# Cross-attention in a perceiver block: steps reordered, and the wide key half changes TensorE column tiles every two batches

## What is computed

```python
def cross_attn(x, context, Wq, Wk, Wv):
    Q = x @ Wq
    K, V = (context @ Wk, context @ Wv)
    energy = jnp.einsum('bqd,bkd->bqk', Q, K)
    Sk = energy.shape[-1]
    lengths = jnp.sum(energy[:, 0] != 0, axis=-1)
    pad = kidx[None, None, :] >= lengths[:, None, None]
    energy = jnp.where(pad, NEG_INF, energy)
    score = jax.nn.softmax(energy / np.sqrt(DK), axis=-1)
    return jnp.einsum('bqk,bkd->bqd', score, V)
```

## Time and profile before

| | |
|---|---|
| median of three runs | 1068.92 us |
| the profiled execution | 1062.33 us, its span 1060.4 us |
| TensorE busy | 1031.4 us, 97% of the span |
| VectorE, ScalarE, GpSimd busy | 577.9, 391.1, 198.7 us |
| granted TensorE clock, mean | 0.994 |
| moved by DMA | 206.93 MB |

### The profile page before, as it was taken

One profiled execution on the slowest core, in us unless ns is written; L12 is line 12 of the kernel. 1 busy time (PEld: TensorE's weight loads), 2 busy tenths in 40 slices (PEclk: granted clock), 3 DMA queues, 4 the chain that ended last, 5 costly groups with the idle time before them and its releaser, 6 DMA issues.

```text
span 1060.4 us, 14025 instructions
## 1 busy us (share of the span) xinstructions
PE 1031.4 (97%) x5263; PEld 768.1 (72%) x5263; DVE 577.9 (55%) x1111; ACT 391.1 (37%) x622; POOL 198.7 (19%) x180
## 2 busy tenths in 40 slices
PE   8999899999999999899999999999999999999998
PEld 4454444444444467788888888899999999999997
DVE  4056333324333448798645666767555665556556
ACT  2111122111111223335567662444444444444441
POOL 2002400000000046535522224630000000000041
PEclk9999999999999989999999999999999999999999
DMA  9934199989999922103421100684554545544453
GB/s 304 400 125 171 77 364 400 380 358 401 416 404 407 377 65 59 40 20 100 126 63 40 40 11 8 230 299 146 179 197 147 187 145 186 184 147 168 145 154 135
DMA packets 38567, 206.93 MB, mean 195 GB/s; under 512 B 5313, under 2 KB 6849, under 8 KB 34289
## 3 DMA queue, kind: packets, MB, share of 16 engines
q1 hardware_dynamic: 33312, 187.98, 48.4%
q0 software_dynamic: 5200, 18.22, 4.8%
HBM read 190.07 MB, written 16.12 MB: 194 GB/s over the span
## 4 chain that ended last, share of the span: by engine, by line
PE 88%; DVE 6%; DMA 2%; POOL 2%; issue 1%; ACT 1%; SPq 0%; DVEq 0%; ACTq 0%
PE ps L632 22%; PE ps L850 21%; PE ps L866 11%; PE ps L559 8%; PE ps L585 8%; PE ps L443 7%; DMA big<-in_ctx 2%; PE ps L463 1%; DVE big L1349 1%; PE ps L543 1%; PE ps L450 1%; PE ps L587 1%; PE ps L891 1%; DVE big L1354 1%; DVE stats L1219 1%; PE ps L569 1%
## 5 line engine op out<-in xcount | busy, mean ns | idle before, releaser
L850 PE MATMUL ps<-x,w 128*128 128x320 f32 x1536 | 237.2, 310 | 1.1 <-DVE x L1750 1.1
L850 PEld LDWEIGHTS ps<-x,w 128*128 128x128 f32 x1536 | 228.5, 188 | 5.1 <-issue 1.4
L1700 DVE TENSOR_TENSOR w<-big,w 128x1536 fp32r<-128x1536 f32 x64 | 112.4, 1758 | 91.7 <-ACT w L1143 91.2
L1805 POOL TENSOR_TENSOR u<-big,u 128x512 fp32r<-128x512 f32 (+1 forms) x44 | 64.0, 1463 | 364.1 <-ACT u L983 364.1
L866 PE MATMUL ps<-w,hsplit 128*128 128x512 f32 x512 | 128.9, 394 | 0.0
L1143 ACT CAST w<-big 128x1536 fp32r<-128x1536 f32 x64 | 94.4, 1478 | 40.2 <-PE ps L866 40.2
L559 PE MATMUL ps<-big 128*64 128x512 f32 (+2 forms) x512 | 103.2, 505 | 2.4 <-DVE ps L1343 1.1
L866 PEld LDWEIGHTS ps<-w,hsplit 128*128 128x128 f32 x512 | 93.3, 188 | 16.6
L632 PE MATMUL ps<-xcT,u 128*128 128x512 f32 x432 | 98.2, 389 | 0.0
L632 PEld LDWEIGHTS ps<-xcT,u 128*128 128x128 f32 x432 | 81.0, 188 | 17.0 <-DVE xcT L1488 0.2
L443 PE MATMUL ps<-big 128*128 128x512 f32 x208 | 90.5, 594 | 0.9 <-ACT big L932 0.9
(11 more groups left out here) (280 smaller groups left out, 1367.7 us busy)
## 6 DMA issues: line engine op xcount, KB each, us to landing
big<-in_ctxT SPq DMA_DIRECT2D x16, 3202.0 KB, 14.2
big<-in_ctx SPq DMA_DIRECT2D x16, 3072.0 KB
big<-in_w_units SPq DMA_DIRECT2D x64, 768.0 KB, 4.3
big<-in_dense_units SPq DMA_DIRECT2D x42, 256.0 KB, 2.7
xs<-big POOLq DMA_DIRECT2D x1, 5120.0 KB, 24.4
big<-in_gate_units SPq DMA_DIRECT2D x12, 384.0 KB, 3.0
hr<-xs SPq DMA_DIRECT2D x7, 512.0 KB, 5.2
ys<-big POOLq DMA_DIRECT2D x7, 512.0 KB, 3.3
```

The lines of the kernel that those rows point to most:

```text
L850: mm = nc.tensor.matmul(ps[:, 2 * part + f % 2, 0:SLOTS], wsplit[f % RING][w][:, c:c + P], xsplit[j][x][:, d, :], start=(d == 0 and w + x ...
L1700: V.tensor_tensor(wsplit[f % RING][1][:], wraw[f % RING], wsplit[f % RING][0][:].bitcast(F32), ALU.subtract).then_inc(w_low, 1)
L1805: G.tensor_tensor(low[:, 0:w], uraw[u % 4][:, 0:w], high[:, 0:w].bitcast(F32), ALU.subtract).then_inc(u_low, 1)
```

## The change

- The wide half sits in column tile 0 for batches 0, 1, 4, 5, ... and in tile 1 for 2, 3, 6, 7, ... (`WIDE`); its matmuls are issued first. The narrow half's pad in PSUM is on the other partitions after each switch, so it is written anew every second batch, with -1e38 instead of 0. Pad columns then count as nonzero, and a small constant `sides` corrects count and key index (one more subtraction in `shift`, and a subtraction in place of a copy in `exchanged`).
- `values` is issued in two parts: its first two key tiles before the exchange, the other four and the tail after.
- The late queries are issued in halves over steps 1 to 7 (`LATE`), the third chunk whole in step 5.
- The output of n-2 is transposed without folding (four 128-column transposes). VectorE then adds the two halves (`output_sum`) between the count and the reading of the exchange, into a buffer that shares memory with two later tiles; ScalarE and VectorE take high and low parts from there.
- The first rows of the product by Wv no longer wait for the outputs of batches 14 and 15; the transposes of batch 15 come after row 1. ScalarE rounds four weight units, not two, ahead of the last output copy.

```diff
@@ -36,6 +36,8 @@
 NEG = -1e38
 FLOOR = -5e37
 PIECES = ((0, 512, 512), (512, KA - 512, KH * P - 512))
+WIDE = [n // 2 % 2 for n in range(B)]
+LATE = {1: (0, 0, 2), 2: (0, 2, 4), 3: (1, 0, 2), 4: (1, 2, 4), 5: (2, 0, 4), 6: (3, 0, 2), 7: (3, 2, 4)}
 ATANH_TERMS = 9
...
-        fold = sb("fold", [P, S])
...
-        oh = sb("oh", [P, NT * TOPK, NE])
-        rk = sb("rk", [P, NT * TOPK, NE])
+        pair = sb("oh_rk", [P, 2, NT * TOPK * NE])
+        oh, rk = (pair[:, k, :].rearrange("p (n e) -> p n e", e=NE) for k in range(2))
+        osum = pair[:].rearrange("p k (c q) -> p (k c) q", q=S)
-        s_work = sb("s_work", [P, 2, 12])
+        s_work = sb("s_work", [P, 2, 13])
+        sides = sb("sides", [P, 2, 4])
...
-            def late_queries(c):
-
-                pe.wait_ge(late_out, 8)
-                if c:
-                    pe.wait_ge(late_q_out, c)
-                for d in range(DC):
+            def late_queries(c, lo, hi):
+
+                if lo == 0:
+                    pe.wait_ge(late_out, 8)
+                    if c:
+                        pe.wait_ge(late_q_out, c)
+                for d in range(lo, hi):
                     mm = nc.tensor.matmul(ps[:, 1, :], m2[:, d, tok(c)], late2T[d], start=(d == 0), stop=(d == DC - 1))
-                mm.then_inc(late_q, 1)
+                if hi == DC:
+                    mm.then_inc(late_q, 1)
...
                 if n:
                     pe.wait_ge(shifted, n)
-                else:
-                    pe.wait_ge(pad_cleared, 1)
+                if n % 2 == 0:
+                    pe.wait_ge(pad_cleared, n // 2 + 1)
                 for piece, (lo, *widths) in enumerate(PIECES):
                     for d in range(DC):
-                        for half in range(2):
-                            col, w = half * KA + lo, widths[half]
+                        for half in (WIDE[n], 1 - WIDE[n]):
+                            narrow = half != WIDE[n]
+                            col, w = narrow * KA + lo, widths[narrow]
                             mm = nc.tensor.matmul(ps[half * S:half * S + S, 2 + piece, 0:w], qT[:, d, n * S:(n + 1) * S],
                                                   cT[n % 2][:, d, col:col + w], start=(d == 0), stop=(d == DC - 1))
                 mm.then_inc(e_done, 1)
...
-            def values(n):
+            def values(n, lo, hi):
 
                 j = n % 2
-                pe.wait_ge(nat_in[j], 32 * (n // 2 + 1))
-                pe.wait_ge(pt_evac[0], n + 1)
-                pe.wait_ge(pt_evac[1], 2 * n + 2)
-                if n:
-                    pe.wait_ge(o_copied, n)
-                for t in range(KH):
-                    for half in range(2):
+                if lo == 0:
+                    pe.wait_ge(nat_in[j], 32 * (n // 2 + 1))
+                    pe.wait_ge(pt_evac[0], n + 1)
+                    if n:
+                        pe.wait_ge(o_copied, n)
+                else:
+                    pe.wait_ge(pt_evac[1], 2 * n + 2)
+                for t in range(lo, hi):
+                    for half in (WIDE[n], 1 - WIDE[n]):
+                        narrow = half != WIDE[n]
                         mm = nc.tensor.matmul(ps[half * S:half * S + S, 6, :], pts[:, t, half * S:half * S + S],
-                                              nat[j][:, half * KH + t, :], start=(t == 0), stop=(half == 1 and t == KH - 1))
-                mm = nc.tensor.matmul(ps[0:S, 6, :], pts[0:TAIL, KH, 0:S], nat[j][0:TAIL, KT, :], start=False, stop=True)
-                mm.then_inc(pv_done, 1)
+                                              nat[j][:, narrow * KH + t, :], start=(t == 0), stop=(narrow and t == KH - 1))
+                if hi == KH:
+                    w = slice(WIDE[n] * S, WIDE[n] * S + S)
+                    mm = nc.tensor.matmul(ps[w, 6, :], pts[0:TAIL, KH, w], nat[j][0:TAIL, KT, :], start=False, stop=True)
+                    mm.then_inc(pv_done, 1)
 
             def transpose_output(n):
 
                 pe.wait_ge(o_copied, n + 1)
                 if n:
-                    pe.wait_ge(o_evac, n)
+                    pe.wait_ge(o_evac, 2 * n - 1)
                 for d in range(DC):
-                    mm = nc.tensor.matmul(ps[:, 7, d * S:(d + 1) * S], osb[:, d * P:(d + 1) * P], fold[:],
-                                          start=True, stop=True)
+                    mm = nc.tensor.transpose(ps[:, 7, d * P:(d + 1) * P], osb[:, d * P:(d + 1) * P], ident[:])
                 mm.then_inc(o_done, 1)
...
                     transpose_probabilities(n - 1)
                 if n >= 2:
                     transpose_output(n - 2)
+                if n:
+                    values(n - 1, 0, 2)
                 exchange(n)
                 if n == 0:
                     late_transposes()
-                if 3 <= n < 3 + DC:
-                    late_queries(n - 3)
+                if n in LATE:
+                    late_queries(*LATE[n])
                 if n:
-                    values(n - 1)
-            transpose_output(B - 1)
+                    values(n - 1, 2, KH)
...
-            pe.wait_ge(o_evac, B)
-            for i in range(6):
+            pe.wait_ge(o_evac, 2 * (B - 2))
+            value_rows(0)
+            value_rows(1)
+            transpose_output(B - 1)
+            value_rows(2)
+            pe.wait_ge(o_evac, 2 * B - 1)
+            for i in range(3, 6):
                 value_rows(i)
             split_transposes("t2", 0)
             split_transposes("t2", 1)
             value_rows(6)
             split_transposes("t2", 2)
             split_transposes("t2", 3)
+            pe.wait_ge(o_evac, 2 * B)
             value_rows(7)
             pe.wait_ge(fb_low, 2)
             fc1_half(0)
...
             def output_out(n):
-                act.wait_ge(o_done, n + 1)
-                nc.scalar.copy(oT_high[:, :, n * S:(n + 1) * S],
-                               ps[:, 7, 0:DC * S].rearrange("p (c q) -> p c q", q=S)).then_inc(o_high, 1)
+                act.wait_ge(o_evac, 2 * n + 1)
+                nc.scalar.copy(oT_high[:, :, n * S:(n + 1) * S], osum[:]).then_inc(o_high, 1)
...
-                    if 3 <= n < 3 + DC:
-                        late_queries_out(n - 3)
+                    if n in LATE and LATE[n][2] == DC:
+                        late_queries_out(LATE[n][0])
                     if n == B:
-                        for u in range(2):
+                        for u in range(DC):
                             unit_high(u)
                     output_copy(n - 1)
                 if n == 3:
                     nc.scalar.copy(fbias[:], lnw[:, 6, :]).then_inc(fb_high, 1)
             output_out(B - 1)
-            for u in range(2, 10):
+            for u in range(DC, 10):
                 unit_high(u)
 
...
-            V.memset(ps[S:P, 3, PIECES[1][2]:PIECES[1][1]], 0.0).then_inc(pad_cleared, 1)
+            def clear_pad(n):
+                rows = slice(S, P) if WIDE[n] == 0 else slice(0, S)
+                V.memset(ps[rows, 3, PIECES[1][2]:PIECES[1][1]], NEG).then_inc(pad_cleared, 1)
+
+            clear_pad(0)
...
                 dve.wait_ge(e_done, n + 1)
+                dve.wait_ge(pad_cleared, n // 2 + 1)
                 V.tensor_scalar(kpad[:, 0:KA], e_cols, 0.0, None, ALU.not_equal,
                                 ALU.add, accum_out=s_cnt[:, n % 2:n % 2 + 1]).then_inc(cnt_done, 1)
...
-                V.tensor_copy(s_stat[:, (n + 1) % 2, 2 + lo:2 + hi], ps[:, 0, lo:hi]).then_inc(misc_read, 1)
+                V.tensor_tensor(s_stat[:, (n + 1) % 2, 2 + lo:2 + hi], ps[:, 0, lo:hi], sides[:, WIDE[n % B], lo:hi],
+                                ALU.subtract).then_inc(misc_read, 1)
                 dve.wait_ge(misc_read, n + 1)
...
+                V.tensor_tensor(c[:, j, 12:13], length, sides[:, WIDE[n], 3:4], ALU.subtract).then_inc(len_step, 1)
                 V.reciprocal(c[:, j, 11:12], length).then_inc(len_step, 1)
-                V.tensor_scalar(kpad[:, 0:KA], kidx[:, 0:KA], length, NEG, ALU.is_ge, ALU.mult).then_inc(len_step, 1)
-                dve.wait_ge(len_step, 3 * n + 2)
+                dve.wait_ge(len_step, 4 * n + 2)
+                V.tensor_scalar(kpad[:, 0:KA], kidx[:, 0:KA], c[:, j, 12:13], NEG, ALU.is_ge, ALU.mult).then_inc(len_step, 1)
+                dve.wait_ge(len_step, 4 * n + 3)
                 V.tensor_tensor(c[:, j, 11:12], c[:, j, 11:12], length, ALU.mult).then_inc(len_step, 1)
...
+                if n % 2 and n + 1 < B:
+                    clear_pad(n + 1)
...
+            def output_sum(n):
+                dve.wait_ge(o_done, n + 1)
+                if n:
+                    dve.wait_ge(o_evac, 2 * n)
+                V.tensor_reduce(osum[:], ps[:, 7, :].rearrange("p (c h q) -> p c q h", h=2, q=S), AX_X,
+                                ALU.add).then_inc(o_evac, 1)
 
             def output_low(n):
                 dve.wait_ge(o_high, n + 1)
                 cols = slice(n % 8 * S, (n % 8 + 1) * S)
```

(24 more changed lines are left out.)

## The result

| | before | changed |
|---|---|---|
| median, 11 runs each | 1069.18 us | 1058.99 us |
| lowest, highest | 1060.32, 1071.44 | 1056.79, 1067.8 |
| profiled execution (span) | 1062.33 (1060.4) | 1065.92 (1064.0) |
| granted clock in it | 0.994 | 0.990 |

The ratio of the times on record is 0.994, 95% interval 0.9911 to 0.997: the change makes the kernel faster, by less than 1%. (The two medians by themselves give 0.990; why they lie further apart comes at the end of the experiments.) The profiled execution of the changed kernel is one of the longest of its 11, longer than that of before. It must therefore be read stage by stage, not by its span.

A forecast was written before the change was run, and what follows sets the result against it. Transfers were taken to bound the batch loop, VectorE to set the pace behind it. Gains of 4.1 and 4.7 sum to 8.8, taking the profiled 1062.3 to 1053.5 and the median 1068.9 to 1060.1 us, range 1050 to 1068.

The forecast's parts named there:

- The bound: Batch loop: transfers, 16.22 us a batch with the DMA full, set its end; TensorE is faster and runs out.
- TensorE's step: Batch loop: a step without a late query goes from 14.51 to 13.7 us (minus 0.76, minus 0.43, plus 0.4).
- 0.4 for two more changes between tiled and untiled matmuls: Each TensorE step: two more such changes cost 0.2 us each, 0.4 together, bounds 0 and 1.0.
- The gain in the loop: End of the batch loop: values of batch 15 may begin 4.1 us earlier, at 366.8, bounds 0 and 6.
- the closing of gaps: Columns of batches 4 to 15: 183.7 us become eleven full intervals, 178.4, so 5.3 come back.
- the early loss: Step 1 of the loop: the half query makes the context load of batch 2 1.2 us later, bounds 0 and 2.
- The step that named the spread late queries as the cause: Early loop steps: half queries make them 15.5 us, below 16.22, instead of 18.05, where the DMA idled.
- Behind the loop: From values of batch 15 to VectorE's row 4: 4.7 us gained, bounds 0.6 and 6.
- VectorE's load, the shift, the queues: Loop steps: VectorE's busy time grows from 5.34 to 6.3 of 14 us, nobody waits; SyncE's load order stays.
- The clock as the slower rival: Steps 12 to 16: waits for loads lower the granted clock, 20 us lost against the gain, 1080 us; chance 0.06.

The follow-up runs named there:

- experiment 3: Whole late queries in steps 3 to 6 instead of halves over steps 1 to 7, in the changed kernel: 1057.46 us, ratio 0.9926 to the kernel before.
- experiment 9: Whole late queries in steps 3 to 6 and the routing stage interleaved with output product chunks, in the changed kernel: 1056.55 us, ratio 0.993 to before.
- experiment 12: Late queries in halves over steps 1 to 7, nothing else, in the kernel before: 1063.08 us, ratio 0.9995 to the kernel before.
- experiment 8: Four of row 6's six output product chunks put between the routing stage's small matmuls, in the changed kernel: 1056.9 us, ratio 0.9948 to before.

## Why the prediction was right

The median came out at 1058.99 where 1060.1 was forecast, within 1% as was likeliest. The forecast was a gain of 8.8; at equal clock it is 4 to 6, and 6.4 by the ratio. That the median came within 1.1 us all the same is luck: the 8.8 were taken off a median of 1068.92 in which low-clock runs weigh (later medians of before were 1063.1 to 1068.6), while nine of the changed kernel's eleven runs had a clock of 0.992 or more. The mechanism held in its main lines, and the sizes were too large, as follows.

- **The bound.** Right for the changed kernel. Its loop ends when the transfers do: leaving row loads out gives it 12.9 us; undoing the alternation gives TensorE 0.43 a step more and moves no landing. In the kernel before the two were nearly level: without the loads its last values start only 1.6 us earlier. So the shorter step was needed to uncover the bound, and could win little before it met it.
- **TensorE's step.** 13.7 forecast, 13.56 measured: values start at 1.55 (1.5), the exchange adds 0.69 (0.5), alternation gives 0.43 (0.43). The forecast without its 0.4 for two more changes between tiled and untiled matmuls is 13.32, so 0.24 of the 0.4 showed up, most of it where the exchange now sits between values. The Trainium skill's drain (TensorEngine Tiling (Array Packing), section Key Properties) may be in these 0.24; no run separates it. Only the alternation was tested alone; what the earlier first part of values gives is read from the timeline.
- **The gain in the loop.** 4.1 forecast. The last columns land 228.0 after the first scores in the old loop (mean of 227.5, 227.5 and 228.9) and 225.1 in the new one (225.7, 224.9, 225.5, 224.9, 224.6): 2.9. Of its terms the closing of gaps was 5.3 and measured about 4.4 (B, 184.3 on average against 179.9), the early loss 1.2 and measured 1.5 (A). The step that named the spread late queries as the cause was wrong: experiments 3 and 9 close the gaps as well without them (B 178.5 and 179.3). The shorter step alone does it. In the kernel before, whose step is long, the spreading does close gaps (experiment 12), but loses 1.5 us in step 1 as everywhere. I had compared each step with 16.22 by itself and had not carried along how far TensorE gets ahead in short steps.
- **Behind the loop.** 4.7 forecast. C gives 3.9 against the profiled execution, of which 1.9 is the clock lost in that profile's pause and 2.5 the new order, less output_sum's price. Take D here as 369.87, the start of values of batch 15. VectorE started row 0 at D + 14.7, not 14.1. TensorE's rows began at D + 6.6 (6.3), the last chunk of row 0 waited 0.2 for GpSimd's fourth low part until 378.87 (the chain shows it), and so output_sum, which follows the transposes of batch 15, began at D + 13.2, not 12.4. From there output_sum and the two evictions took 1.5 (1.6 forecast).
- **VectorE's load, the shift, the queues.** Right, with one small wait: output_sum took 0.69, VectorE is busy for 6.21 us of the window 257 to 271 (6.3 forecast), and TensorE waited for the shift only before the scores of batch 1, 0.63 us where it had been 0.42. SyncE's rows of batch 2 went out 1.6 later relative to the first scores (1.2).
- **The clock as the slower rival.** Did not come in the loop: with waits of 0.4 to 1.8 us in steps 11 to 15 the clock stayed at 1.00, in all profiles with the reordered steps. The Trainium skill's kernel whose clock falls at each wait for a transfer (TensorE: Matmul & The Clock Gate, section HAM oscillation) is not met here. But a fall of the clock in the routing stage, where no transfer is waited for, which I had left out and whose cause stays open, moves the time by 8 us and more from run to run, more than the change.

## What to carry to other kernels

When a busy engine's loop is fed by transfers, compare the step with the transfer of a step before costing anything: here 13.1 us of TensorE time in the loop bought about 3, since TensorE and the transfers were nearly level before. Then look at what delays the first load of the loop, since everything behind it moves along. When the profile of a faster kernel is longer than that of the slower one, compare marks stage by stage and the granted clock of the runs; what the clock loses behind a pause or among small-column matmuls can be more than an edit gives.

A version that does better than both has the changed kernel's steps with whole late queries in steps 3 to 6 (experiments 3 and 9): ratios of 0.9926 and 0.993 to before, with loops 2 to 3.5 us shorter than the changed one. The intervals overlap with the changed kernel's 0.994. The landings show it to be better; of the times only a hint does: at a clock of 0.997 or 0.998 the four such runs of experiment 3 took 1054.3 on average and the changed kernel's five 1057.5, but experiments 8 and 9 differ by 0.4 us there (1057.2 and 1056.8).

## What the runs showed of the hardware that I had not expected

- The clock can fall while TensorE is shown as busy. In the window from 652 to 656 us of the changed kernel it is busy for 4.00 of 4 us, with transposes and products of 8 columns, and the clock went to 0.72 and then 0.50; just ahead, from 650 to 652, it was busy for 1.78 of 2 us at 1.00. The same instructions in the profile of before, with the same idle 0.2 us ahead of them (1.76 of 2 us busy from 652 to 654), kept 1.00. Between the changed kernel's two profiles the stretch from the first dense product to the end differs by 8.5 us (662.2 and 653.7). By their mean clocks (0.990 and 0.997 over the span) some 7.5 of these are clock, an estimate.
- Column tiles work side by side, and their loads can be balanced: with the tail and the next wide half on different tiles the next transposes start 6.12 us after the tail, on the same tile 6.55. The gain is one of the tail's two passes of 0.43, as forecast. That the tail and the next scores start together (258.84 both) is no sign of it, since they do so with one side too (264.70 and 264.71 in the earlier trace rows).
